# Eight Toeplitz products per middle block instead of ten, and the second block's residual in four pieces

## Chip, core and metric

The kernel runs on one core of a Trainium2 chip. The metric is the device time of one execution in microseconds (us). Before the change the median of three runs is 409.83 us, from 409.52 to 410.25 us.

## What is computed

The input is 2 x 1024 rows of 512 float32 values. Each row is normalised. One branch convolves it causally with a learned kernel K of 512 taps (an S4 layer, whose K is built on the chip from small complex vectors); the other is a gated feed-forward layer with low-rank (LoRA) additions to its weights. The result is their product added to the input:

```python
xn = _layernorm(x, axis=-1)
# s: causal convolution of xn with K along the 512 values, plus D * xn
y = jnp.fft.irfft(jnp.fft.rfft(u, n=n) * jnp.fft.rfft(K, n=n), n=n)[..., :L]
s = y + D[0] * u
# g: silu of the feed-forward layer
h1 = _lora_linear(x, w1, lora_A1, lora_B1)
h3 = _lora_linear(x, w3, lora_A3, lora_B3)
f = _lora_linear(silu(h1) * h3, w2, lora_A2, lora_B2)
x = x + s * silu(f)
```

## The kernel before

The 2048 rows are worked on in four blocks of 512 rows. Features lie on the partitions, in four chunks of 128 (c = 0 to 3), and rows along the free axis. A float32 product is made of three matmuls on values split into a high and a low part (fp32r): low weights by high data, high weights by low data, high by high. The function `three` issues them, and its three lines in the profile are L991, L992 and L993. Each streams 512 columns.

**A block.** The 1376 hidden units are 11 tiles, j = 0 to 10. For a tile TensorE makes `gate` into bank h1 (12 matmuls), `up` into bank h3 (12 matmuls), and then `down(j-1)`, the product of the previous tile's hidden values with w2, into four banks f (12 matmuls). Between them ScalarE applies silu to h1 (L651), VectorE multiplies by h3 (L837), ScalarE makes the high part `ghl[0]` with a cast (`hidden_hi`, L668) and VectorE the low part `ghl[1]` with a subtraction (`hidden_lo`, L842). There is one buffer `ghl`, so `hidden_hi` of tile j waits on the semaphore g_used until `down(j-1)` has read it. Each engine runs its instructions in the order of its own program; in the bodies of ScalarE and VectorE that order is told by the places "gate", "up" and "down" of each j. `hidden_lo(j)` stands at (j, "up").

**The convolution.** K is 512 taps, so the convolution is a lower triangular Toeplitz matrix of 4 x 4 chunks. With T0 to T3 for its four different chunks, kept split in `tzs`, output chunk c is the sum of T(c-i) by x(i) for i = 0 to c: 4 + 3 + 2 + 1 = 10 products, 30 matmuls. `convolve` makes them at the end of each block, into the banks h1, h3, spare1 and spare0, among the last `down` products (`down_chunk` of tile 10). `out_sum` on VectorE multiplies them with silu of f and adds the residual `xres`.

**Blocks.** Block 0 is written out and also builds the folded weights: raw tiles of w1, w3 and w2 are loaded, a low-rank product from TensorE is added, and the sum is split. Blocks 1 and 2, the middle blocks, are one loop body, and block 3 is written out. The next block's data is prepared during a block: moments on VectorE (L792, L795), their reciprocal roots on GpSimd (`rows_rstd`), a store and a broadcast load of the scales, `next_scale` on GpSimd (four tensor_tensor of 128x512), `next_shift` on VectorE (L819), the high part on ScalarE (L637) and the low part on VectorE (`next_lo`, L823).

**Queues.** Nearly all loads are issued by SyncE (SP) in one written order. The residual of block 1 is one transfer of 1 MB (`load_residual(1, 1)`), issued ahead of the last six raw weight tiles; `next_scale(1, 1)` waits for it. At the end of a middle block SP stores the four output chunks, and then loads the rows of the next but one.

Of the kernel before, what the change touches and what calls it, by code (L numbers as in the profile page):

```python
# [25 lines left out]
ALU = mybir.AluOpType  # L26
# [18 lines left out]

COS, MASK, SIGN, MINUS_HALF, EULER, MINUS_ONE, EPSILON, EYE = 0, 8, 10, 11, 13, 14, 18, 20

# [163 lines left out]


def spare_uses():
# [32 lines left out]
def s4_constants():  # L246

    L = D  # L250
    lane = np.arange(L // 2)
    mirror = np.where(lane == 0, L // 2, L - lane)
    l = np.concatenate([lane, mirror])
    half = np.pi * l / L
    trig = np.concatenate([np.sin(half), np.cos(half)])[None, :].astype(np.float32)
    cosc = np.repeat(np.cos(half).reshape(4, P).T, 2, axis=1)
    mask = np.ones((P, 2))
    mask[0, 0] = 0.0
    sign = np.where(np.arange(P) < NS, 1.0, -1.0)[:, None]
    powers = np.tile([-0.5, -0.5, np.e, -1.0, -1.0, -1.0, -1.0, EPS, EPS], (P, 1))  # L260
    lanes = np.concatenate([cosc, mask, sign, powers, np.eye(P)], axis=1).astype(np.float32)
    t = np.arange(L) + 0.5
    lc, ls = lane, np.where(lane == 0, L // 2, lane)
    cos_rows = np.cos(2 * np.pi * ((lc[:, None] * t[None, :]) % L) / L) / L
    sin_rows = -np.sin(2 * np.pi * ((ls[:, None] * t[None, :]) % L) / L) / L
    dft = np.stack([cos_rows, sin_rows]).reshape(2, 2, P, P, K_PARTS).transpose(3, 4, 0, 2, 1).reshape(P, K_PARTS, L).astype(np.float32)
    return trig, lanes, np.ascontiguousarray(dft)


def build(nc, x, xT, w1, w3, w2, lora, lora_early, lora_late, s4_lanes, s4_vc, s4_bp, s4_scalars, trig, lanes, dft, outT):  # L270
    ctx = ExitStack()
    with ctx:
# [25 lines left out]
        xn = put("xn", [P, RT, D])  # L298
        g = put("g", [P, BLK])
        tz = put("tz", [P, D])  # L300
        lane_c = put("lane_c", [P, EYE + P])
# [3 lines left out]
        scales = put("scales", [P, 2, RT])  # L305
        bp_sb = put("bp_sb", [P, NS])
        scal = put("scal", [P, 2])
# [8 lines left out]
        coef = put("coef", [P, 4])  # L316
        kcol = put("kcol", [P, K_PARTS])
        assert base + top[0] <= nc.sbuf_usable_end

# [26 lines left out]
        rows_next = at("rows_next", [P, 2, D], lora_off + (DC + 2) * BLK * 4)  # L346
        scale_rows = at("scale_rows", [P, 2, BLK], lora_off + (DC + 4) * BLK * 4)
        assert lora_off + (DC + 6) * BLK * 4 <= xn_off

# [63 lines left out]
        s4_step = sem("s4_step")  # L413
        pads_cleared = sem("pads_cleared")


# [79 lines left out]
        def wait_residual(eng, b):  # L496
            if isinstance(b, int) and b == 0:
                eng.wait_ge(res0_in, 16)
            else:
                eng.wait_ge(res_in, 16 * b)  # L500

# [9 lines left out]
        def _(sync):  # L511
# [111 lines left out]
        def _(act):  # L623
# [61 lines left out]
            def out_gate(b):  # L685
                for n, c in enumerate(OUT_ORDER):
# [4 lines left out]
                    nc.scalar.activation(gate[:, n % 2, :], f[c][:, :], ACT.Silu).then_inc(gate_done, 1)  # L691

            def body(b, par_next, first, last):
                norm_at = NORM_AT_FIRST if first else NORM_AT
# [29 lines left out]
                if last:  # L724
                    last_gate(b)
                else:
                    out_gate(b)


# [28 lines left out]
        def _(dve):  # L758
# [86 lines left out]
            def last_sum(b, par):  # L845
# [3 lines left out]
                for i, (n, out, cols) in enumerate(steps):  # L849
                    part = gate_last(n)[:, cols]  # L850
                    dve.wait_ge(gate_done, b * DC + n + 1)
                    dve.wait_ge(conv_ready, b * DC + i + 1)
# [3 lines left out]
                    nc.vector.tensor_tensor(sum_, sum_, part, ALU.add).then_inc(res_done, 1)  # L856

            def out_sum(b, par):
# [13 lines left out]
            def body(b, par, par_next, first, last):  # L872
                norm_at = NORM_AT_FIRST if first else NORM_AT
                split_at = SPLIT_AT_FIRST if first else SPLIT_AT
                moments_at = MOMENTS_AT_FIRST if first else MOMENTS_AT
                late = []
# [45 lines left out]
                if last:  # L922
                    last_sum(b, par)
                else:
                    out_sum(b, par)
# [28 lines left out]
        def _(pe):  # L954
# [118 lines left out]
            def convolve(b, par, c_out, first):  # L1073
# [12 lines left out]
                mm.then_inc(conv_ready, 1)  # L1086

            def convolve_halves(b, par, c_out):

# [22 lines left out]
            def body(b, par, first, last):  # L1112
                if first:
                    start()
                for j in range(1 if first else 0, HT):
# [5 lines left out]
                    else:  # L1121
                        pe.wait_ge(conv_used, (b - 1) * DC + 1)
                    if j == HT - 1:
# [9 lines left out]
                    else:  # L1133
                        pe.wait_ge(conv_used, (b - 1) * DC + 2)
                    if j == HT - 1:
# [41 lines left out]
        def _(pool):  # L1177
# [28 lines left out]
            def next_scale(b, par):  # L1206

                pool.wait_ge(scale_rows_in, 16 * b)
                pool.wait_ge(res_in, 16 * b)
                for c in range(DC):  # L1210
# [137 lines left out]
            pool.wait_ge(wlo_done, len(DVE_LO))  # L1348
            next_scale(1, 1)
            with pool.Fori(1, NBLK - 1) as b:  # L1350
                for r in range(0, RT, 2):
                    rows_rstd(b + 1, r)
                pool.wait_ge(conv_ready, b * DC)
                next_scale(b + 1, (b + 1) % 2)
# [55 lines left out]
```

## Time and profile before

| | value |
|---|---|
| median of 3 runs (range) | 409.83 us (409.52 to 410.25) |
| profiled execution | 409.98 us |
| its span in the trace | 408.2 us |
| mean granted TensorE clock | 0.999 of full speed |
| busy: TensorE / its weight loads / VectorE / ScalarE / GpSimd | 403.3 / 335.8 / 170.1 / 105.9 / 73.3 us |

The span is the stretch from the first to the last instruction in the trace, and lies 1.8 us under the execution's own time. The busy time of TensorE counts each matmul from its start to its modelled end; one matmul's end lies behind the next one's start, so the cost of a matmul is read from start to start. PE is TensorE, PEld its weight loads, DVE VectorE, ACT ScalarE, POOL GpSimd and SP SyncE.

### The profile page before, as it was taken

To read this page: it belongs to the slowest core of one execution; us is meant where nothing else is said; L and a number is where in the kernel's file an instruction comes from. 1 tells how busy PE (TensorE), PEld (TensorE's weight loads), DVE (VectorE), ACT (ScalarE), POOL (GpSimd) and SP (SyncE) were. 2 spreads that over 40 slices of the span, in tenths; PEclk is the share of its full clock that TensorE was granted. 3 is DMA by queue.
4 is the path that set the end of the run, shared out by engine and by line. 5 is a ranking of instruction groups with operands and counts; after the bars stand their busy time and mean duration, and the time that the engine had idled before them with its cause. 6 is when DMAs were issued, how large, how long until landed. Compare 5 with 4: busy or idle time off the path is not lost.

```text
span 408.2 us, 5004 instructions
## 1 busy us (share of the span) xinstructions
PE 403.3 (99%) x1850; PEld 335.8 (82%) x1850; DVE 170.1 (42%) x267; ACT 105.9 (26%) x175; POOL 73.3 (18%) x139
## 2 busy tenths in 40 slices
PE   8999999999999999999999999999999999999996
PEld 8988888887788888888888888888888888888885
DVE  5887776794793322232343221233234111211125
ACT  7554232222351111221221111112222111111122
POOL 6685645402500114000000103300000000000000
PEclk9999999999999999999999999999999999999999
DMA  8573755604425101000016101000002000000002
GB/s 269 166 184 108 231 156 152 171 26 90 145 78 180 52 2 51 2 0 0 2 51 205 53 0 52 0 0 0 0 0 103 2 0 0 2 0 0 2 0 103
DMA packets 14466, 26.89 MB, mean 66 GB/s; under 512 B 2768, under 2 KB 4528, under 8 KB 14320
## 3 DMA queue, kind: packets, MB, share of 16 engines
q1 hardware_dynamic: 13440, 24.53, 19.2%
q0 software_dynamic: 720, 1.60, 2.0%
q10 hardware_dynamic: 288, 0.52, 0.3%
q8 instruction: 11, 0.18, 0.2%
q14 instruction: 7, 0.06, 0.1%
HBM read 21.45 MB, written 4.54 MB: 64 GB/s over the span
## 4 chain that ended last, share of the span: by engine, by line
PE 94%; DVE 3%; issue 1%; DMA 1%; ACT 1%; POOL 0%; DVEq 0%; POOLq 0%
PE h L991 20%; PE h L992 20%; PE h L993 20%; PE f L991 10%; PE f L992 10%; PE f L993 10%; PE h L1014 2%; PE spare L978 1%; DMA xn<-x_dram 1%; DVE raw L768 1%; PE spare L993 1%; PE spare L973 1%; PE spare L992 1%; PE spare L991 1%; DVE w L783 0%
## 5 line engine op out<-in xcount | busy, mean ns | idle before, releaser
L991 PE MATMUL h<-xt,w 128*128 (+2 forms) x340 | 131.4, 386 | 0.0
L992 PE MATMUL h<-xt,w 128*128 (+2 forms) x340 | 131.2, 386 | 0.0
L993 PE MATMUL h<-xt,w 128*128 (+2 forms) x340 | 131.2, 386 | 0.0
L991 PEld LDWEIGHTS h<-xt,w 128*128 128x128 f32 x340 | 63.9, 188 | 13.3 <-DVE w L780 0.4
L993 PEld LDWEIGHTS h<-xt,w 128*128 128x128 f32 x340 | 63.9, 188 | 12.9
L992 PEld LDWEIGHTS h<-xt,w 128*128 128x128 f32 x340 | 63.9, 188 | 12.3
L837 DVE TENSOR_TENSOR g<-g,h 128x512 f32<-128x512 f32 x40 | 27.5, 686 | 106.3 <-PE h L993 106.1
L842 DVE TENSOR_TENSOR ghl<-g,ghl 128x512 fp32r<-128x512 f32 x44 | 32.4, 736 | 90.0 <-ACT ghl L668 90.0
L991 PE MATMUL f<-ghl,w2f 128*128 128x512 f32 x176 | 68.8, 391 | 0.0
L992 PE MATMUL f<-ghl,w2f 128*128 128x512 f32 x176 | 68.6, 390 | 0.0
L993 PE MATMUL f<-ghl,w2f 128*128 128x512 f32 x176 | 68.5, 389 | 0.0
L668 ACT CAST ghl<-g 128x512 fp32r<-128x512 f32 x44 | 27.3, 621 | 155.6 <-PE f L993 145.0
L991 PEld LDWEIGHTS f<-ghl,w2f 128*128 128x128 f32 x176 | 33.0, 188 | 7.0 <-issue 0.4
L993 PEld LDWEIGHTS f<-ghl,w2f 128*128 128x128 f32 x176 | 33.1, 188 | 7.0
L992 PEld LDWEIGHTS f<-ghl,w2f 128*128 128x128 f32 x176 | 33.1, 188 | 6.5
L651 ACT ACTIVATE g<-h 128x512 f32<-128x512 f32 x40 | 23.9, 597 | 44.9 <-PE h L993 44.9
L1190 POOL TENSOR_TENSOR scales<-moments,lane_c 128x2 f32<-128x2 f32 x6 | 1.5, 256 | 120.6 <-DVE moments L795 120.6
L768 DVE SCALAR_TENSOR_TENSOR raw<-spare,raw 128x512 f32<-128x512 f32 (+2 forms) x33 | 22.3, 675 | 2.0 <-DVE raw L768 1.1
L628 ACT CAST w<-raw 128x512 fp32r<-128x512 f32 (+1 forms) x22 | 13.4, 610 | 30.4 <-DVE raw L768 30.4
L1190 POOL TENSOR_TENSOR normal_rows<-xres,scale_rows 128x512 f32 (+1 forms) x12 | 16.1, 1372 | 19.8 <-DMA scale_rows<-scales_scratch 19.8
L783 DVE TENSOR_TENSOR w<-raw,w 128x512 fp32r<-128x512 f32 (+1 forms) x17 | 13.0, 772 | 0.3 <-DVE raw L768 0.2
L637 ACT CAST xt<-normal_rows (+1 forms) x12 | 7.4, 621 | 16.4 <-DVE normal_rows L819 16.4
(141 smaller groups left out, 310.4 us busy)
## 6 DMA issues: line engine op xcount, KB each, us to landing
raw<-w_dram SPq DMA_DIRECT2D x28, 256.0 KB, 3.9
xres<-xT_dram SPq DMA_DIRECT2D x4, 1024.0 KB, 6.9
outT_dram<-xres SPq DMA_DIRECT2D x15, 256.0 KB, 2.5
rows_next<-x_dram SPq DMA_DIRECT2D x4, 512.0 KB, 3.6
scale_rows<-scales_scratch SPq DMA_DIRECT2D x3, 512.0 KB, 4.2
rows<-x_dram SPq DMA_DIRECT2D x2, 512.0 KB, 7.1
dft_sb<-dft_dram SPq DMA_DIRECT2D x1, 1024.0 KB, 5.0
raw<-w_dram SPq DMA_DIRECT2D x4, 224.0 KB, 3.2
```

The costliest lines, as they stand in the source:

```text
L628: nc.scalar.copy(folded(kind, j, 0), raw_tile(kind, j)).then_inc(whi_done, 1)
L651: nc.scalar.activation(g[:, :], h1[:, :], ACT.Silu).then_inc(silu_done, 1)
L668: nc.scalar.copy(ghl[:, 0, :], g[:, :]).then_inc(ghi_done, 1)
L768: nc.vector.scalar_tensor_tensor(out=rt, in0=low, scalar=LORA_SCALE, in1=rt, op0=ALU.mult, op1=ALU.add) \
L783: nc.vector.tensor_tensor(folded(kind, j, 1), raw_tile(kind, j), folded(kind, j, 0).bitcast(F32), ALU.subtract).then_inc(wlo_done, 1)
L837: nc.vector.tensor_tensor(g[:, :], g[:, :], h3[:, :], ALU.mult).then_inc(g_done, 1)
L842: nc.vector.tensor_tensor(ghl[:, 1, :], g[:, :], ghl[:, 0, :].bitcast(F32), ALU.subtract).then_inc(glo_done, 1)
L991: pe.matmul(out, w[1], m[0], start=start, stop=False)
L992: pe.matmul(out, w[0], m[1], start=False, stop=False)
L993: return pe.matmul(out, w[0], m[0], start=False, stop=stop)
L1014: mm = pe.matmul(h3[:, :], joint[:, c, JOINT_APART:JOINT_APART + P], xt[:, par, hl, c, :], start=(c == 0 and hl == 1), stop=(c == DC - 1 a ...
L1190: return nc.gpsimd.tensor_tensor(out, a, c, op)
```

## The change

In blocks 1 and 2 the ten products are replaced by eight, in the manner of Karatsuba. With P0 = T0 x0, P1 = T1 x1 and P2 = T2 x2, the chunks are

- y0 = P0
- y1 = (T0+T1)(x0+x1) - P0 - P1
- y2 = (T0+T2)(x0+x2) - P0 - P2 + P1
- y3 = T3 x0 + T0 x3 + (T1+T2)(x1+x2) - P1 - P2

TensorE makes them at four places of the block (`products`, behind `down(j-1)` of j = 2, 4, 5 and 6) and at its end (`last_product`). VectorE forms the sums of x (`pair_sum`: three additions each), ScalarE casts them (`pair_high`), VectorE subtracts (`pair_low`), and `mix` combines the products. The sums of T are formed once, on GpSimd and ScalarE, between block 0 and block 1. Blocks 0 and 3 keep their ten products. The load of block 1's residual becomes four transfers of 256 KB, each behind one of the raw tiles.

The diff, without the allocations, the semaphores and the wait counts of the last block:

```diff
+MIX_AT = {(3, "gate"): (0,), (5, "gate"): (1,), (6, "gate"): (2,), (7, "gate"): (3,)}
+PAIRS = ((0, 1), (0, 2), (1, 2))
+PAIR_AT, PAIR_LO_AT = {(4, "gate"): 0, (5, "gate"): 1, (7, "gate"): 2}, {(4, "up"): 0, (5, "up"): 1, (7, "up"): 2}
...
 @@ sync
+            def load_residual_part(c):
+                sync.dma_start(resid(1, c), xT[:, c, BLK:2 * BLK]).then_inc(res_in, 16)
...
             sync.wait_ge(xt_turned, RT)
-            load_residual(1, 1)
-            for kind, j in later[17:]:
+            for n, (kind, j) in enumerate(later[17:]):
                 load_raw(kind, j)
+                if n < DC:
+                    load_residual_part(n)
...
 @@ scalar
+            def pair_high(b, k):
+                act.wait_ge(pair_step, 9 * b - 9 + 3 * k + 3)
+                nc.scalar.copy(pair_hi[:, :], pair_f[:, :]).then_inc(pair_cast, 1)
+            def mid_gate(b):
+                for n, c in enumerate(OUT_ORDER):
+                    e = b * DC + n
+                    act.wait_ge(f_ready, e + 1)
+                    act.wait_ge(res_done, e - 1)
+                    nc.scalar.activation(scale_rows[:, n % 2, :], f[c][:, :], ACT.Silu).then_inc(gate_done, 1)
...
                         if place == "gate" and not (first and j == 0):
                             hidden(b, j)
+                        if mid and (j, place) in PAIR_AT:
+                            if PAIR_AT[j, place] == 0:
+                                act.wait_ge(tsum_done, 2)
+                            pair_high(b, PAIR_AT[j, place])
...
                 else:
                     out_gate(b)
+                    act.wait_ge(tsum_added, 2)
+                    nc.scalar.copy(tsum[:, 0, :, :], tsum_f[:, :, :]).then_inc(tsum_hi, 1)
+                    nc.scalar.copy(t12_hi[:, :], t12_f[:, :]).then_inc(tsum_hi, 1)
...
 @@ vector
+            def pair_sum(b, par, k):
+                lo, hi = [[xt[:, par, hl, c, :].bitcast(F32) for c in PAIRS[k]] for hl in (1, 0)]
+                n = 9 * b - 9 + 3 * k
+                whole = pair_f[:, :]
+                nc.vector.tensor_tensor(whole, lo[0], lo[1], ALU.add).then_inc(pair_step, 1)
...
+                nc.vector.tensor_tensor(whole, whole, hi[0], ALU.add).then_inc(pair_step, 1)
...
+                nc.vector.tensor_tensor(whole, whole, hi[1], ALU.add).then_inc(pair_step, 1)
+            def pair_low(b, k):
+                dve.wait_ge(pair_cast, 3 * b - 3 + k + 1)
+                nc.vector.tensor_tensor(pair_lo[:, :], pair_f[:, :], pair_hi[:, :].bitcast(F32), ALU.subtract) \
+                    .then_inc(pair_ready, 1)
+            def mix(b, stage):
+                p, m, s = PRODUCTS * b - PRODUCTS, PRODUCTS * b - PRODUCTS, 3 * b - 3
+                dve.wait_ge(prod_ready, p + stage + 1)
+                if stage == 0:
+                    nc.vector.tensor_copy(y2, sp[1][:, :]).then_inc(mix_step, 1)
...
+                    nc.vector.tensor_tensor(y1, sp[0][:, :], y2, ALU.add).then_inc(mix_done, 1)
...
+            def mid_sum(b, par):
+                mix(b, 4)
+                dve.wait_ge(mix_done, PRODUCTS * b)
+                wait_residual(dve, b)
+                sums = {3: less, 2: y2, 1: y1, 0: sp[0][:, :]}
...
                     for place in ("gate", "up", "down"):
+                        if mid:
+                            for stage in MIX_AT.get((j, place), ()):
+                                mix(b, stage)
+                            if (j, place) in PAIR_AT:
+                                pair_sum(b, par, PAIR_AT[j, place])
                         if place == "up" and not (first and j == 0):
                             hidden_mul(b, j)
...
                         if place == "up":
                             hidden_lo(b, j)
+                        if mid and (j, place) in PAIR_LO_AT:
+                            pair_low(b, PAIR_LO_AT[j, place])
...
 @@ tensor
+            def paired(b, k, out, start, stop):
+                pe.wait_ge(pair_ready, 3 * b - 3 + k + 1)
+                t = [t12_hi[:, :], t12_lo[:, :]] if k == 2 else [tsum[:, hl, k, :] for hl in (0, 1)]
+                return three(out, t, [pair_hi[:, :], pair_lo[:, :]], start, stop)
+            def products(b, par, j):
+                m = PRODUCTS * b - PRODUCTS
+                if j == 2:
+                    single(b, par, 0, take(b, ("conv", b, 0), False)[:, :])
+                    single(b, par, 1, take(b, ("conv", b, 1), False)[:, :]).then_inc(prod_ready, 1)
+                if j == 4:
+                    pe.wait_ge(mix_done, m + 1)
+                    pe.wait_ge(tsum_done, 2)
+                    paired(b, 0, sp[1][:, :], True, True).then_inc(prod_ready, 1)
+                if j == 5:
+                    pe.wait_ge(mix_done, m + 2)
+                    single(b, par, 2, sp[1][:, :]).then_inc(prod_ready, 1)
+                if j == 6:
+                    pe.wait_ge(mix_done, m + 3)
+                    paired(b, 1, sp[1][:, :], True, True).then_inc(prod_ready, 1)
+            def last_product(b, par):
+                pe.wait_ge(mix_done, PRODUCTS * b - PRODUCTS + 4)
+                three(sp[1][:, :], lag(3), [xt[:, par, hl, 0, :] for hl in (0, 1)], True, False)
+                three(sp[1][:, :], lag(0), [xt[:, par, hl, 3, :] for hl in (0, 1)], False, False)
+                paired(b, 2, sp[1][:, :], False, True).then_inc(prod_ready, 1)
...
                         down(b, j - 1)
                     if first:
                         extras(j, "down")
+                    elif not last:
+                        products(b, par, j)
...
+                if not first:
+                    last_product(b, par)
+                    down_wait(b, HT - 1)
+                    for c in OUT_ORDER:
+                        down_chunk(HT - 1, c).then_inc(f_ready, 1)
+                    return
...
 @@ gpsimd
             next_scale(1, 1)
+            pool.wait_ge(tz_in, 16)
+            once = tz[:, 0:P].rearrange("p (a l) -> p a l", a=1).to_broadcast([P, 2, P])
+            tt(tsum_f[:, :, :], tz[:, P:3 * P].rearrange("p (a l) -> p a l", a=2), once, ALU.add).then_inc(tsum_added, 1)
+            tt(t12_f[:, :], tz[:, P:2 * P], tz[:, 2 * P:3 * P], ALU.add).then_inc(tsum_added, 1)
+            pool.wait_ge(tsum_hi, 2)
+            tt(tsum[:, 1, :, :], tsum_f[:, :, :], tsum[:, 0, :, :].bitcast(F32), ALU.subtract).then_inc(tsum_done, 1)
+            tt(t12_lo[:, :], t12_f[:, :], t12_hi[:, :].bitcast(F32), ALU.subtract).then_inc(tsum_done, 1)
```

## Rows read from the trace of the kernel before

**Rows 1.** The page, busy time by engine (share of the span) and TensorE's granted clock in 40 slices

```profile
PE 403.3 (99%) x1850; PEld 335.8 (82%) x1850; DVE 170.1 (42%) x267; ACT 105.9 (26%) x175; POOL 73.3 (18%) x139
...
PEclk9999999999999999999999999999999999999999
```

**Rows 2.** Windows of blocks 1 and 2: start:end, length, busy (count), clock, DMA share, GB/s

```profile
117.73:213.28 95.55, 95.55 (x423) 79.12 (x422) 31.22 (x51) 20.43 (x34) 7.63 (x12) 1.00 0.13 42
213.28:308.93 95.65, 95.65 (x423) 79.22 (x422) 29.23 (x48) 19.35 (x33) 7.60 (x12) 1.00 0.12 39
```

**Rows 3.** Waits of block 2: who waited for whom, total us, times, longest

```profile
ACT ghl L668 <- PE f L993: 45.7, 10, 4.8
```

**Rows 4.** Timeline in block 2, TensorE, ScalarE and VectorE where down(3) ends: start, us, instruction

```profile
251.36 0.39 PE L991 MATMUL h<-xt,w 128*128 x1
...
251.56 0.62 ACT L668 CAST ghl<-g 128x512 fp32r<-128x512 f32 x1 [4.84 <-PE f L993]
...
252.22 0.69 DVE L842 TENSOR_TENSOR ghl<-g,ghl 128x512 fp32r<-128x512 f32 x1 [2.62 <-ACT ghl L668]
```

**Rows 5.** Timeline of VectorE in block 2, hidden_lo(5) with the next instruction behind it

```profile
260.38 0.69 DVE L842 TENSOR_TENSOR ghl<-g,ghl 128x512 fp32r<-128x512 f32 x1 [2.62 <-ACT ghl L668]
260.99 0.69 DVE L819 TENSOR_TENSOR normal_rows<-normal_rows,scale_rows 128x512 f32 x1
```

**Rows 6.** Timeline in block 0 where TensorE waits for VectorE

```profile
94.08 0.28 DVE L780 TENSOR_TENSOR w<-raw,w 128x128 fp32r<-128x128 f32 x1
...
94.46 0.47 PE L991 MATMUL h<-xt,w 128*128 128x512 f32 x1
...
94.77 0.39 PE L992 MATMUL h<-xt,w 128*128 128x512 f32 x1
```

**Rows 7.** Timeline of GpSimd, its next_scale in block 0 and in block 2

```profile
108.66 1.29 POOL L1190 TENSOR_TENSOR normal_rows<-xres,scale_rows 128x512 f32<-128x512 f32 x1
109.91 1.74 POOL L1190 TENSOR_TENSOR normal_rows<-xres,scale_rows 128x512 f32<-128x512 f32 x1
...
253.31 5.04 POOL L1190 TENSOR_TENSOR normal_rows<-xres,scale_rows 128x512 f32 x4 [6.03 <-DMA scale_rows<-scales_scratch]
```

**Rows 8.** Timeline of VectorE at the end of block 0

```profile
108.68 1.82 DVE L842 TENSOR_TENSOR ghl<-g,ghl 128x512 fp32r<-128x512 f32 x1 [1.14 <-ACT ghl L668]
110.42 1.77 DVE L819 TENSOR_TENSOR normal_rows<-normal_rows,scale_rows 128x512 f32<-128x512 f32 x1
112.11 0.68 DVE L819 TENSOR_TENSOR normal_rows<-normal_rows,scale_rows 128x512 f32<-128x512 f32 x1
...
116.50 0.68 DVE L863 TENSOR_TENSOR gate<-gate,h 128x512 f32<-128x512 f32 x1
```

**Rows 9.** Timeline of TensorE at the first instruction of block 1

```profile
117.48 0.19 PEld L991 LDWEIGHTS h<-xt,w 128*128 128x128 f32 x1 [0.17 <-issue]
117.57 0.41 PE L991 MATMUL h<-xt,w 128*128 x1
```

**Rows 10.** Timeline at the end of block 1: tile 10's low part, TensorE's first convolution and down_chunk

```profile
204.62 0.69 DVE L842 TENSOR_TENSOR ghl<-g,ghl 128x512 fp32r<-128x512 f32 x1 [0.91 <-ACT ghl L668]
...
203.76 0.39 PE L991 MATMUL h<-xt,tzs 128*128 x1
...
206.48 0.39 PE L991 MATMUL f<-ghl,w2f 128*128 128x512 f32 x1
```

**Rows 11.** Timeline of VectorE across the boundary at 213.28: out_sum and the next block's first product

```profile
210.71 0.69 DVE L863 TENSOR_TENSOR gate<-gate,h 128x512 f32<-128x512 f32 x1 [0.95 <-ACT gate L691]
211.54 0.69 DVE L869 TENSOR_TENSOR xres<-xres,gate 128x512 f32 x1
...
218.99 0.69 DVE L837 TENSOR_TENSOR g<-g,h 128x512 f32<-128x512 f32 x1 [3.04 <-PE h L993]
```

**Rows 12.** Timeline of the SP queue in block 0 around the residual of block 1

```profile
67.06 0.66 SPq L548 DMA_DIRECT2D xres<-xT_dram  x1
69.05 27.66 SPq L543 DMA_DIRECT2D raw<-w_dram  x6
```

More of the change, by code:

```diff
@@ L260, in s4_constants @@
     powers = np.tile([-0.5, -0.5, np.e, -1.0, -1.0, -1.0, -1.0, EPS, EPS], (P, 1))
-    lanes = np.concatenate([cosc, mask, sign, powers, np.eye(P)], axis=1).astype(np.float32)
+    lanes = np.concatenate([cosc, mask, sign, powers, np.ones((P, 4)), np.eye(P)], axis=1).astype(np.float32)
     t = np.arange(L) + 0.5
@@ L299, in build @@
         g = put("g", [P, BLK])
+        tz_off = (top[0] + 31) // 32 * 32
         tz = put("tz", [P, D])
+        lane_c_off = (top[0] + 31) // 32 * 32
         lane_c = put("lane_c", [P, EYE + P])
@@ L317, in build @@
         kcol = put("kcol", [P, K_PARTS])
+        assert bp_off + P * 4 <= top[0]
+        sum_off = (top[0] + 31) // 32 * 32
+        tsum = put("tsum", [P, 2, 2, P], F32R)
+        tsum_f = at("tsum_whole", [P, 2, P], sum_off + 2 * P * 4)
+        t12_hi = at("t12_hi", [P, P], lane_c_off + EYE * 4, F32R)
+        t12_lo = at("t12_lo", [P, P], bp_off, F32R)
+        t12_f = at("t12_whole", [P, P], bp_off)
         assert base + top[0] <= nc.sbuf_usable_end
@@ L347, in build @@
         scale_rows = at("scale_rows", [P, 2, BLK], lora_off + (DC + 4) * BLK * 4)
+        pair_f = at("pair_whole", [P, BLK], lora_off + (DC + 3) * BLK * 4)
+        pair_lo = at("pair_lo", [P, BLK], lora_off + (DC + 3) * BLK * 4, F32R)
+        pair_hi = at("pair_hi", [P, BLK], tz_off, F32R)
+        y1, y2, less = gate[:, 0, :], gate[:, 1, :], rows_next[:, 0, :]
         assert lora_off + (DC + 6) * BLK * 4 <= xn_off
@@ L414, in build @@
         pads_cleared = sem("pads_cleared")
+        tsum_added, tsum_hi, tsum_done = sem("tsum_added"), sem("tsum_hi"), sem("tsum_done")
+        prod_ready, mix_step, mix_done = sem("prod_ready"), sem("mix_step"), sem("mix_done")
+        pair_step, pair_cast, pair_ready = sem("pair_step"), sem("pair_cast"), sem("pair_ready")
         joint = w13[:, W13_AT[1, JOINT] // 4:W13_BYTES // 4].rearrange("p (c u) -> p c u", c=DC)
@@ L691, in out_gate @@
                     nc.scalar.activation(gate[:, n % 2, :], f[c][:, :], ACT.Silu).then_inc(gate_done, 1)
+            def pair_high(b, k):
[7 more added lines that the diff above has]
+                    nc.scalar.activation(scale_rows[:, n % 2, :], f[c][:, :], ACT.Silu).then_inc(gate_done, 1)
             def body(b, par_next, first, last):
+                mid = not first and not last
                 norm_at = NORM_AT_FIRST if first else NORM_AT
@@ new lines, in pair_low @@
+            def pair_low(b, k):
[7 more added lines that the diff above has]
+                    nc.vector.tensor_copy(y2, sp[1][:, :]).then_inc(mix_step, 1)
+                    dve.wait_ge(mix_step, s + 1)
+                    nc.vector.tensor_tensor(y1, sp[0][:, :], y2, ALU.add).then_inc(mix_done, 1)
+                if stage == 1:
+                    dve.wait_ge(mix_done, m + 1)
+                    nc.vector.tensor_tensor(y1, sp[1][:, :], y1, ALU.subtract).then_inc(mix_done, 1)
+                if stage == 2:
+                    nc.vector.tensor_tensor(less, y2, sp[1][:, :], ALU.add).then_inc(mix_step, 1)
+                    nc.vector.tensor_tensor(y2, y2, sp[1][:, :], ALU.subtract).then_inc(mix_done, 1)
+                    dve.wait_ge(mix_done, m + 3)
+                    nc.vector.tensor_tensor(y2, y2, sp[0][:, :], ALU.subtract).then_inc(mix_step, 1)
+                if stage == 3:
+                    dve.wait_ge(mix_step, s + 3)
+                    nc.vector.tensor_tensor(y2, y2, sp[1][:, :], ALU.add).then_inc(mix_done, 1)
+                if stage == 4:
+                    dve.wait_ge(mix_step, s + 3)
+                    nc.vector.tensor_tensor(less, sp[1][:, :], less, ALU.subtract).then_inc(mix_done, 1)
@@ new lines, in mid_sum @@
+            def mid_sum(b, par):
[3 more added lines that the diff above has]
+                sums = {3: less, 2: y2, 1: y1, 0: sp[0][:, :]}
+                for n, c in enumerate(OUT_ORDER):
+                    e = b * DC + n
+                    part = scale_rows[:, n % 2, :]
+                    dve.wait_ge(gate_done, e + 1)
+                    nc.vector.tensor_tensor(part, part, sums[c], ALU.mult).then_inc(conv_used, 1)
+                    dve.wait_ge(conv_used, e + 1)
+                    if c < 2:
+                        dve.sem_inc(spare_free[c], 1)
+                    nc.vector.tensor_tensor(resid(par, c), resid(par, c), part, ALU.add).then_inc(res_done, 1)
@@ L875, in body @@
                 moments_at = MOMENTS_AT_FIRST if first else MOMENTS_AT
+                mid = not first and not last
                 late = []
@@ L923, in body @@
                     last_sum(b, par)
+                elif mid:
+                    mid_sum(b, par)
                 else:
@@ L1086, in convolve, with lag, single @@
                 mm.then_inc(conv_ready, 1)
+            def lag(d):
+                return [tzs[:, hl, d * P:(d + 1) * P] for hl in (0, 1)]
+            def single(b, par, d, out):
+                return three(out, lag(d), [xt[:, par, hl, d, :] for hl in (0, 1)], True, True)
+            def paired(b, k, out, start, stop):
[22 more added lines that the diff above has]
+                paired(b, 2, sp[1][:, :], False, True).then_inc(prod_ready, 1)
             def convolve_halves(b, par, c_out):
```

22 lines of the change are left out of this document (15 added, 7 removed).

## Prediction

> **What bounds the kernel.** I read the page's busy times first: TensorE is busy 99% of the span at the full granted clock in every slice, VectorE 42%, ScalarE 26%, GpSimd 18% [rows 1]. A busy share alone does not show that TensorE is fed without gaps, because its matmuls overlap in the record. So I took the windows of the two middle blocks next. They are bounded by the starts of two successive first matmuls, and in the second, 95.65 us hold 422 weight loads [rows 2]: 95.65 / 422 = 0.2267 us from matmul to matmul. The same spacing stands in the timeline wherever I looked in these blocks, so block 2 has no idle time of TensorE at all. The consequence for the reader is double. Every matmul taken out of such a block is worth 0.227 us, and every wait put in front of a matmul is paid in full, unless it is moved under other matmuls: nothing in the block absorbs it. So the question of this change is only whether the new operands are ready when TensorE comes to them.
>
> **What is removed.** Ten products become eight, each of three matmuls: 6 matmuls a block, 12 in all, 12 x 0.2267 = 2.72 us less. (The Trainium skill, page "TensorE: Matmul & The Clock Gate", section "Back-to-back issue gap", gives about 216 ns for an isolated gap of 512 columns and 131 ns for a sustained stream; by the latter the twelve would be worth 1.57 us. The rows here show 227 ns, and decide.)
>
> **What is added on TensorE's path: the first paired product.** For each product I compared the point in TensorE's program with the point at which its operand is made.
>
> `paired(0)` stands right behind `down(3)`, in `products` of j = 4. It waits for pair_ready, which `pair_low` increments. `pair_low(0)` stands on VectorE at (4, "up"), behind `hidden_lo(4)`, and that waits for the cast of `hidden_hi(4)`. The cast waits for g_used, since `ghl` is a single buffer: it can't run before `down(3)` has read it. The waits show just this: ten times in the block the cast waits for TensorE's f product, 4.8 us at the longest [rows 3]. In the timeline the matmul behind `down(3)` starts at 251.36 and the cast at 251.56 [rows 4]. So where before the next matmul (gate of tile 5) needed nothing of this chain, TensorE now waits for all of it. The links, from the moment at which the next matmul would have started:
>
> - to the start of the cast 251.56 - 251.36 = 0.20 us, and from the cast to the subtraction 252.22 - 251.56 = 0.66 us [rows 4]
> - from `hidden_lo` to the next instruction of VectorE 260.99 - 260.38 = 0.61 us, which now is `pair_low`, and 0.69 us for it, as a tensor_tensor of the same form takes [rows 5]
> - from VectorE's end to TensorE's matmul 94.46 - 94.36 = 0.10 us, and 0.31 instead of 0.23 us to the second matmul after a wait, 0.08 us [rows 6]
>
> Together 2.34 us in each middle block, 4.68 us in all. The nearest bounds: without the restart 2.26 us a block; with `pair_low` behind one instruction of GpSimd, 3.5 us (rival B). What hangs behind the stall shifts as a whole, because the chain of later tiles starts from TensorE too.
>
> **The other products are covered.** `single` 0 and 1 at j = 2 need only x. `mix(0)` then has the gate and up products of tile 3 (24 matmuls, 5.4 us) before VectorE must multiply by h3. `single(2)` at j = 5 waits for `mix(1)`, which has a whole tile (36 matmuls, 8.16 us). `pair_sum(1)` and `mix(1)` are four instructions of 0.69 us, 2.8 us with some 0.1 us between them, and VectorE owes nothing to tile 5 until its gate and up products are through, 5.4 us after the stall. `paired(1)` needs `pair_low(1)`, made behind `down(4)`, and is used behind `down(5)`: 8.16 us for some 2.3 us. `paired(2)` has three tiles. So they cost nothing as long as VectorE is not late by more than a tile.
>
> **End of a block.** Tile 10's low part is ready at 204.62 + 0.69 = 205.31, and `down(9)` gives way at 203.76. Before, 12 matmuls of convolution covered that until 206.48 [rows 10]. Now nine do, until 203.76 + 9 x 0.2267 = 205.80: the wait stays covered with 0.5 us to spare. `mid_sum` starts later against the block's end, since all four f products come last: four pairs of instructions at some 1.5 us (0.83 us from product to sum, then the next), from about 1.2 us before the boundary to 4.9 us after it. The next thing VectorE has to do is at 218.99, 5.7 us after 213.28 [rows 11]. Covered, and if not, the h3 bank isn't needed before 8.2 us. SP's stores and the next rows' load come about 2 us later; the rows are read by moments that nobody needs for several tiles.
>
> **Between blocks 0 and 1: the sums of T.** GpSimd adds 256 and 128 columns right behind `next_scale(1, 1)`, which ends at 109.91 + 1.74 = 111.65 [rows 7], while VectorE works without a pause toward L863, which ends at 117.18. TensorE's first load of block 1 waits for that product (h1 is a convolution bank there) and starts at 117.48 [rows 9]: 0.30 us of slack. Where GpSimd's 512-column instructions overlap VectorE's with two SBUF inputs, these take 1.82 and 1.77 us instead of 0.68 or 0.69, about 1.1 us more each, and end about when GpSimd's do [rows 7, 8]. Scaled by columns, the two new ones cost VectorE 0.55 + 0.28 = 0.83 us. Less the slack, plus 0.1 us of restart, TensorE loses 0.6 us, once. Bounds: 0 if they fall in gaps; 1.9 us if both cost as much as one of 512 columns. I take the scaled value, since the length of an elementwise instruction goes with its columns. (The Trainium skill, page "SBUF — State Buffer", section "Who interferes with whom", has a rule against this change: a VectorE instruction with two SBUF inputs and a GpSimd one that reads SBUF exclude each other for a whole instruction. The trace agrees: 1.82 against 0.69 us. Without that rule the term would be 0.) The casts on ScalarE and GpSimd's subtractions come behind `out_gate(0)` and are wanted at j = 4 of block 1, 30 us later.
>
> **The residual in pieces.** The 1 MB transfer goes out at 67.06, and the six raw tiles from 69.05 to 96.7 [rows 12]; their issues wait for earlier splits. The pieces go out behind the first four, the last one before the sixth tile at 96.7, and GpSimd reads the residual in the `next_scale` that is under way at 108.66 [rows 7]. The view of waits lists no fold that waited for a raw tile's transfer, so the raw tiles gain nothing by coming sooner. Zero, hidden on both sides.
>
> **Sum.** -2.72 + 4.68 + 0.6 = +2.56 us. Against the profiled execution's 409.98 us this is 412.54; that execution lies 0.15 us above the median, so I forecast 412.4 us.
>
> **Rivals.**
>
> - A, the forecast: a stall of some 2.3 us in each middle block, 412.4 us, by its own bounds 411.2 to 413.7. Chance 0.76.
> - B, `pair_low(0)` is caught behind GpSimd. It starts at 252.22 + 0.61 = 252.83, and `next_scale` at 253.31 [rows 7]; both keep their place relative to `down(2)` and `down(3)`, so `pair_low` is first by 0.5 us. If scales land earlier, it loses 1.1 us in each block: 414.6 us. Chance 0.08.
> - C, the granted clock falls after the stall. The clock is full in every slice [rows 1], but no middle block shows an idle TensorE, so no row speaks to 2.3 us. At half the clock, 12 matmuls cost 2.72 us more, in both blocks 5.4 us: 417.8 us, more if it lasts. Against it: block 0 has short waits at a full clock. Chance 0.05.
> - D, the other side: the operand is there in time and the change does what it says. Then -2.72 + 0.6 gives 407.7 us. It would need VectorE to run `pair_low(0)` ahead of `hidden_lo(4)`, or the cast not to wait for `down(3)`; program order and [rows 3] speak against both. It decides as soon as the chain costs less than (2.72 - 0.6) / 2 = 1.06 us a block, less than cast and subtraction alone. Chance 0.07.
> - E, a smaller stall for a reason I don't see, about even with before. Chance 0.04.
>
> **Numbers.** The range 411.2 to 414.0 holds A and the nearer half of B, 0.80. A measurement of this kernel tells about 0.2%, 0.8 us, from no change. Slower by more than that: A, B, C, 0.89. Faster: D, 0.07. Within: E, 0.04.
>
> **What the profile after would show.** The middle blocks hold 416 weight loads instead of 422 and last 95.65 - 1.36 + 2.34 = 96.6 us. TensorE has one idle stretch of about 2.3 us in each, in front of the first matmul that reads `tsum`, with VectorE's `pair_low` as releaser, and none at j = 2, 5, 6 or the end. The first load of block 1 comes some 0.6 us later against the end of block 0, with L863 delayed by GpSimd's additions. The forecast is wrong if `pair_low(0)` ends before `down(3)` does, or if a second idle stretch appears in the block.

## The result and the profile after

The changed kernel takes 415.16 us in the median of six runs (413.62 to 415.93), the kernel before 409.77 us in its six. The ratio is 1.0115, with a 95% interval of 1.0097 to 1.0133: 4.7 us slower, 4.0 to 5.4. The two medians lie 5.4 us apart, at the upper end of that. The forecast was 412.4 us in a range of 411.2 to 414.0: the direction was right, and the measured median lies 2.8 us above the forecast. Two slow executions among the experiments, of 446.5 us (experiment 1, clock 0.852) and 1054.6 us (experiment 2), are left out of the ratios.

The page of the profiled execution (415.93 us, span 414.1 us), its busy times and TensorE's granted clock:

```profile
PE 405.0 (98%) x1838; PEld 336.5 (81%) x1838; DVE 200.0 (48%) x307; ACT 110.0 (27%) x183; POOL 81.3 (20%) x143
...
PEclk9999999999999998999999999899999999999999
```

Against [rows 1] twelve matmuls are gone, VectorE is busy for 30 us more, and the clock, full in every slice before, has two slices with an 8. The view of waits of TensorE, in total us, times, longest (pair_lo is written by `pair_low`, gate by L972):

```profile
PE spare L1110 <- DVE pair_lo L926: 4.1, 2, 2.0
PE h L1141 <- POOL g L1376: 1.0, 1, 1.0
PE h L1110 <- DVE gate L972: 0.7, 1, 0.7
```

The wait for GpSimd's g stands in the kernel before too, with the same 1.0 us. The two new waits, the first and the third, are the ones that the forecast named. The first, in block 1, in the timeline of TensorE, ScalarE and VectorE (L702 is the cast, L897 hidden_lo, L926 pair_low, L1110 to L1112 the three lines of `three`):

```profile
157.38 0.39 PE L1112 MATMUL f<-ghl,w2f 128*128 128x512 f32 x1
159.80 0.50 PE L1110 MATMUL spare<-pair_hi,tsum 128*128 128x512 f32 x1 [2.03 <-DVE pair_lo L926]
160.14 0.40 PE L1111 MATMUL spare<-pair_lo,tsum 128*128 128x512 f32 x1
...
157.81 0.62 ACT L702 CAST ghl<-g 128x512 fp32r<-128x512 f32 x1 [2.71 <-PE f L1112]
...
158.46 0.69 DVE L897 TENSOR_TENSOR ghl<-g,ghl 128x512 fp32r<-128x512 f32 x1 [2.61 <-ACT ghl L702]
159.06 0.68 DVE L926 TENSOR_TENSOR pair_lo<-pair_whole,pair_hi 128x512 fp32r<-128x512 f32 x1
```

The next matmul would have started at 157.38 + 0.23 = 157.61. It starts at 159.80, 2.19 us late, and the second one comes 0.34 us behind it in place of 0.23: 2.30 us. The chain is cast, subtraction, subtraction, as in [rows 4, 5]. Block 2 repeats it to the hundredth.

What the sum did not hold comes just after the product, in the timeline of TensorE, in block 1 and then in block 2:

```profile
160.38 0.41 PE L1112 MATMUL spare<-pair_hi,tsum 128*128 128x512 f32 x1
160.61 0.60 PE L1110 MATMUL h<-xt,w 128*128 x1
161.01 0.63 PE L1111 MATMUL h<-xt,w 128*128 x1
...
163.57 0.61 PE L1111 MATMUL h<-xt,w 128*128 x1
163.99 0.42 PE L1112 MATMUL h<-xt,w 128*128 x1
164.25 0.40 PE L1110 MATMUL h<-xt,w 128*128 x1
```

```profile
258.14 0.50 PE L1110 MATMUL spare<-pair_hi,tsum 128*128 128x512 f32 x1 [2.03 <-DVE pair_lo L926]
...
259.41 0.44 PE L1112 MATMUL h<-xt,w 128*128 x1
259.65 0.63 PE L1110 MATMUL h<-xt,w 128*128 x1
260.07 0.63 PE L1111 MATMUL h<-xt,w 128*128 x1
```

From 160.61 to 163.99 eight matmuls start 0.40 to 0.43 us apart instead of 0.23. They read the same tiles with the same columns as in [rows 4]. The slow stretch does not begin when the wait ends: it begins 0.8 us after the product's first matmul in block 1 and 1.5 us after it in block 2 (259.65 - 258.14), and the matmuls in between come at the usual spacing. Windows of that stretch and of the two middle blocks (length, busy times, clock):

```profile
160.58:164.36 3.78, 3.78 (x11) 2.93 (x10) 3.36 (x4) 0.00 (x0) 3.78 (x3) 0.55 0.00 0
...
118.01:216.51 98.50, 96.47 (x417) 79.27 (x417) 43.87 (x67) 21.47 (x37) 10.58 (x14) 0.98 0.12 38
216.51:314.87 98.36, 96.33 (x417) 79.13 (x416) 44.41 (x68) 21.13 (x35) 9.32 (x12) 0.98 0.11 37
```

The granted clock of the stretch is 0.55: for most of it TensorE ran at the lower of its two levels, 1.2 GHz, after an idle stretch of 2.0 us. The blocks last 98.50 and 98.36 us. Against the forecast 96.6 us, each is 1.8 to 1.9 us longer. Most of that is the slow stretch: in both blocks the 30 matmuls behind the product's first take 1.8 us more than 30 x 0.2267 us, and in the block of the third run that kept its clock (experiment 7) 0.14 us more. So one fall of the clock costs 1.6 us.

The start of block 1, and VectorE and GpSimd ahead of it:

```profile
118.01 0.50 PE L1110 MATMUL h<-xt,w 128*128 x1 [0.68 <-DVE gate L972]
...
109.20 3.48 DVE L874 TENSOR_TENSOR normal_rows<-normal_rows,scale_rows 128x512 f32<-128x512 f32 x2
112.61 1.22 DVE L878 TENSOR_TENSOR xt<-normal_rows,xt 128x512 fp32r<-128x512 f32 x1
...
117.03 0.68 DVE L972 TENSOR_TENSOR gate<-gate,h 128x512 f32<-128x512 f32 x1
...
112.09 1.19 POOL L1353 TENSOR_TENSOR tsum_whole<-tz 128x256 f32<-128x256 f32 x1
113.24 0.91 POOL L1353 TENSOR_TENSOR t_whole<-tz 128x128 f32<-128x128 f32 x1
```

GpSimd's two additions lie at 112.09 and 113.24, L972 starts at 117.03 instead of 116.50 [rows 8], and block 1 at 118.01 instead of 117.57 [rows 9].

With that the whole difference of the two profiled executions is placed. The window of block 1 in [rows 2] opens 0.16 us after the block's first matmul. From first matmul to first matmul it lasts 213.28 - 117.57 = 95.71 us. Block 1 starts 0.44 us later, lasts 98.50 - 95.71 = 2.79 us longer, and block 2 lasts 98.36 - 95.65 = 2.71 us longer. That is 5.94 of the 5.95 us between 409.98 and 415.93.

### The profile page after: what moved, and what is told of

Its sections match the earlier page's. It is cut to its first block, busy times and chain, and to the rows that moved or that the text cites. A ratio compares the mean times of both kernels' runs of the same rounds, so it can differ in the third digit from the quotient of the medians.

```text
span 414.1 us, 5084 instructions
## 1 busy us (share of the span) xinstructions
PE 405.0 (98%) x1838; PEld 336.5 (81%) x1838; DVE 200.0 (48%) x307; ACT 110.0 (27%) x183; POOL 81.3 (20%) x143
## 4 chain that ended last, share of the span: by engine, by line
PE 92%; DVE 4%; ACT 1%; issue 1%; DMA 1%; POOL 0%; DVEq 0%; ACTq 0%; POOLq 0%
PE h L1110 19%; PE h L1111 19%; PE h L1112 19%; PE f L1110 9%; PE f L1111 9%; PE f L1112 9%; PE h L1133 2%; PE spare L1097 1%; DVE normal_rows L874 1%; PE spare L1110 1%; PE spare L1112 1%; PE spare L1111 1%; DMA xn<-x_dram 1%; PE spare L1092 1%; DVE xt L878 1%
## 5 line engine op out<-in xcount | busy, mean ns | idle before, releaser
L1110 PE MATMUL h<-xt,w 128*128 (+2 forms) x340 | 132.9, 391 | 0.7 <-DVE gate L972 0.7
L1112 PE MATMUL h<-xt,w 128*128 (+2 forms) x340 | 132.2, 389 | 0.0
L1110 PEld LDWEIGHTS h<-xt,w 128*128 128x128 f32 x340 | 64.5, 190 | 14.7 <-issue 1.1
L1112 PEld LDWEIGHTS h<-xt,w 128*128 128x128 f32 x340 | 64.7, 190 | 13.3
L1111 PEld LDWEIGHTS h<-xt,w 128*128 128x128 f32 x340 | 64.7, 190 | 12.7
L897 DVE TENSOR_TENSOR ghl<-g,ghl 128x512 fp32r<-128x512 f32 x44 | 31.0, 704 | 90.4 <-ACT ghl L702 90.4
L1110 PE MATMUL f<-ghl,w2f 128*128 128x512 f32 x176 | 68.7, 390 | 0.0
L1112 PE MATMUL f<-ghl,w2f 128*128 128x512 f32 x176 | 68.5, 389 | 0.0
L702 ACT CAST ghl<-g 128x512 fp32r<-128x512 f32 x44 | 27.3, 621 | 145.6 <-PE f L1112 135.0
L1112 PEld LDWEIGHTS f<-ghl,w2f 128*128 128x128 f32 x176 | 33.0, 188 | 7.0
L1110 PEld LDWEIGHTS f<-ghl,w2f 128*128 128x128 f32 x176 | 33.0, 188 | 6.7
L1353 POOL TENSOR_TENSOR normal_rows<-xres,scale_rows 128x512 f32 (+1 forms) x12 | 19.2, 1628 | 20.7 <-DMA scale_rows<-scales_scratch 20.7
```

What stands on the lines that cost most here:

```text
L702: nc.scalar.copy(ghl[:, 0, :], g[:, :]).then_inc(ghi_done, 1)
L897: nc.vector.tensor_tensor(ghl[:, 1, :], g[:, :], ghl[:, 0, :].bitcast(F32), ALU.subtract).then_inc(glo_done, 1)
L1110: pe.matmul(out, w[1], m[0], start=start, stop=False)
L1111: pe.matmul(out, w[0], m[1], start=False, stop=False)
L1112: return pe.matmul(out, w[0], m[0], start=False, stop=stop)
L1353: return nc.gpsimd.tensor_tensor(out, a, c, op)
```

## Experiments

All ten kernels are timed against the kernel before, in up to five rounds. Where a number of executions by clock is given, it is the mean granted clock that each execution's record shows.

**1. The operand ahead of the cast.** One instruction of the change is moved on VectorE:

```diff
+                        if mid and (j, place) == (4, "up"):
+                            pair_low(b, 0)
                         if place == "up" and not (first and j == 0):
                             hidden_mul(b, j)
...
-                        if mid and (j, place) in PAIR_LO_AT:
+                        if mid and (j, place) in PAIR_LO_AT and j != 4:
```

> The change, with one instruction moved: VectorE runs pair_low(0) at (4, "up") ahead of hidden_mul(4), so that it no longer stands behind the cast of tile 4. Theory A (a stall of 2.30 us in each middle block for pair_low, and behind it some nine matmuls at 0.43 instead of 0.23 us): both vanish together, TensorE idles nowhere in the middle blocks, the granted clock stays full, and the time is that of before -2.72 us for twelve matmuls +0.44 us for GpSimd's additions, about 2.3 us under before. Rival (VectorE or GpSimd are now too loaded and would hold TensorE elsewhere): another idle stretch appears and the time stays at or above that of before.

Measured: ratio 0.9953 (0.9940 to 0.9965), 1.9 us faster than before, 1.4 to 2.5. Its timeline, VectorE and TensorE in block 1:

```profile
154.25 0.69 DVE L926 TENSOR_TENSOR pair_lo<-pair_whole,pair_hi 128x512 fp32r<-128x512 f32 x1 [0.69 <-ACT pair_hi L729]
154.86 0.68 DVE L892 TENSOR_TENSOR g<-g,h 128x512 f32<-128x512 f32 x1
157.59 0.69 DVE L897 TENSOR_TENSOR ghl<-g,ghl 128x512 fp32r<-128x512 f32 x1 [2.04 <-ACT ghl L702]
...
156.50 0.40 PE L1114 MATMUL f<-ghl,w2f 128*128 128x512 f32 x1
156.74 0.39 PE L1112 MATMUL spare<-pair_hi,tsum 128*128 128x512 f32 x1
```

`pair_low` ends at 154.94, and the product follows `down(3)` at the usual spacing, 156.50 to 156.74. The executions in the comparison kept a clock of 0.999 or 1.000. So the place of one subtraction of 0.69 us is the whole difference between 4.7 us slower and 1.9 us faster. The other products and the end of the block put no idle stretch into the middle blocks. This order is the one that rival D of the forecast supposed: it gave 407.7 us, 2.1 us under before.

**2. The idle stretch filled.** Eight matmuls whose result is overwritten:

```diff
                     pe.wait_ge(tsum_done, 2)
+                    for _ in range(8):
+                        pe.matmul(sp[1][:, :], tzs[:, 0, 0:P], xt[:, par, 0, 0, :], start=True, stop=True)
                     paired(b, 0, sp[1][:, :], True, True).then_inc(prod_ready, 1)
```

> The change, with eight extra matmuls of 512 columns into the spare1 bank in front of the wait for pair_low(0); their results are overwritten by the product. They take 1.8 us of the 2.3 us in which TensorE idled. Theory that the fall of the granted clock is a cost of its own, caused by the idle stretch: the stall ends at the same moment, the clock stays full in every execution, and the time is 1.5 to 3.5 us under that of the change, 2.2 to 2.7 us over before. Rival (the slow matmuls come from the reads of the pair or of tsum, or from VectorE's and GpSimd's load, and not from the idle stretch): the matmuls behind the product stay slow and the time is that of the change, 5.4 us over before.

Measured: 1.0065 (1.0052 to 1.0078), 2.7 us slower than before, 2.1 to 3.2. TensorE in its block 2:

```profile
255.70 0.50 PE L1110 MATMUL spare<-pair_hi,tsum 128*128 128x512 f32 x1 [0.23 <-DVE pair_lo L926]
...
257.19 0.40 PE L1110 MATMUL h<-xt,w 128*128 x1
257.42 0.39 PE L1111 MATMUL h<-xt,w 128*128 x1
```

The wait is still there, now 0.23 us of idling behind 1.8 us of filler. The same product, operands and gate matmuls follow, and none is slow in either block; the executions in the comparison show 0.999 or 1.000. Matmuls whose results nobody uses make the changed kernel about 2 us faster. That settles two things: the slow matmuls come from the idle stretch, not from the operands; and without a fall of the clock the change costs 2.7 us, where the forecast had summed 2.56.

**3. and 4. The wait without the change.** The kernel before, with one line. First behind `down(3)`, then behind `down(2)`:

```diff
+                    elif not last and j == 4:
+                        pe.wait_ge(glo_done, b * HT + 5)
```

> The kernel before, with nothing of the change but a wait: behind down(3) in the middle blocks TensorE waits for hidden_lo(4). The links read before give 0.20 + 0.66 + 0.69 + 0.18 = 1.7 us a block. Theory A without a fall of the clock: 3.4 us over before. If so short an idle stretch lowers the granted clock too, up to 1.75 us more in each block, 5 to 7 us over before. Rival (something downstream absorbs the wait): under 2 us over before.

```diff
+                    elif not last and j == 3:
+                        pe.wait_ge(moments_ready, (b + 1) * RT + RT)
```

> The kernel before, with nothing of the change but a longer wait: behind down(2) in the middle blocks TensorE waits for the moments that VectorE takes behind hidden_lo(3), 2.6 us a block, a little more than the 2.3 us of the change. Stall alone: 5.3 us over before. Stall and clock: the granted clock falls behind it as in the change, 1.75 us a block more where it does, up to 8.8 us over before. Rival (the fall of the clock belongs to the paired product's operands): the clock stays full and the time is 5.3 us over before.

Measured: 1.0097 (1.0082 to 1.0112) for the short wait, 4.0 us slower, 3.4 to 4.6; and 1.0172 (1.0145 to 1.0200) for the long one, 7.0 us, 5.9 to 8.2. The matmuls around each wait, in block 1, the short wait first:

```profile
155.66 0.39 PE L993 MATMUL f<-ghl,w2f 128*128 128x512 f32 x1
157.48 0.50 PE L991 MATMUL h<-xt,w 128*128 x1 [1.43 <-DVE ghl L842]
157.81 0.39 PE L992 MATMUL h<-xt,w 128*128 x1
```

```profile
147.24 0.39 PE L993 MATMUL f<-ghl,w2f 128*128 128x512 f32 x1
150.08 0.49 PE L991 MATMUL h<-xt,w 128*128 x1 [2.45 <-DVE moments L795]
150.41 0.40 PE L992 MATMUL h<-xt,w 128*128 x1
```

The short wait costs 157.48 - 155.66 - 0.23 + 0.10 = 1.69 us a block, 3.4 us in all, at the lower end of what the times say; the traces show nothing that would make it 4.0. The long wait costs 150.08 - 147.24 - 0.23 + 0.10 = 2.71 us a block. All four executions with the short wait kept a clock of 1.000. The six with the long one fall on steps: three at 1.000 took 414.8 to 415.4 us, one at 0.996 took 417.0, two at 0.992 took 418.2 and 418.4. The three at 1.000 are 5.4 us over before, twice 2.7; each step down is some 1.6 us, the price of one fall as read above. The kept trace is of an execution at 1.000 and has no slow matmul, so the steps are read from times and mean clocks alone. A wait is paid in full here, and the loss of clock is a second, separate cost that comes in some executions. It needs nothing of the Toeplitz products.

**5. Less filling.** As experiment 2, with `range(3)`, so that 1.36 us stay idle.

> The change with three extra matmuls ahead of the wait for pair_low(0) in place of eight, so that TensorE idles 1.4 to 1.6 us in each middle block instead of 2.0 us. The stall ends at the same moment, so the time without a fall of the clock is that of the version with eight, 412.3 us. Theory that the length of the idle stretch decides about the clock, as the pure wait of 1.6 us without a fall suggests: the clock stays full in all or nearly all executions. Rival (any wait in this place can lower it): executions at 0.991 to 0.996 and a median of 413.5 us or more.

Measured: 1.0075 (1.0061 to 1.0089), 3.1 us slower, 2.5 to 3.6. Four executions at 1.000 took 412.1 to 412.7 us, one at 0.998 took 413.2. None fell to 0.996. The one at 0.998 is 0.5 to 1.1 us over the others; executions of the kernel before at 0.998 took 409.4 to 409.8 us, no more than the rest, so it is open whether that one holds a short fall. In the other four, three matmuls in the gap were enough to keep the clock.

**6. and 7. The change again, twice.**

> The change as it is, once more. Theory A with the clock: two stalls of 2.3 us and GpSimd's term of 0.4 us give 2.3 us over before in an execution whose granted clock stays full, and each fall of the clock adds 1.1 to 1.8 us, so that the executions fall on steps by their mean granted clock (1.000, 0.996, 0.991). Rival: executions at 1.000 also lie more than 3 us over before, and something beside stall and clock costs time.

> The change a third time, for more executions at each mean granted clock. One execution so far kept the full clock and yet took 413.6 us, where stall and GpSimd's term alone give 412.3 us, which is what the version with eight filling matmuls took. Theory A with the clock: further executions at 1.000 lie near 412.3 us, those at 0.995 near 414.2 us and those at 0.991 near 415.7 us. Rival: executions at 1.000 lie at 413.6 us again, and 1.3 us have another cause.

Measured: 1.0101 (1.0085 to 1.0116) and 1.0110 (1.0094 to 1.0125). By their ratios these two are 4.1 and 4.5 us slower than before. With the first six, 14 executions of the change are now sorted by clock: four at 0.990 or 0.991 took 415.5 to 415.9 us, nine at 0.994 to 0.996 took 413.5 to 414.7 us, and one at 1.000 took 413.6 us. The profile of the last run shows one fall, so both prices are in one trace. Windows of its two middle blocks:

```profile
117.48:215.93 98.45, 96.42 (x417) 79.27 (x417) 44.66 (x67) 21.57 (x37) 10.06 (x14) 0.98 0.12 38
215.93:312.66 96.73, 94.69 (x418) 78.03 (x417) 44.21 (x68) 21.11 (x35) 9.35 (x12) 1.00 0.12 38
```

Both blocks have the stall of 2.04 us idle. The one with a full clock lasts 96.73 us, and the forecast for it was 96.6. The one with the fall lasts 1.72 us more. Some 0.1 us of that is the late second matmul at the start of block 1 and not the fall: in experiment 1, which has no fall, block 1 lasts 94.51 us and block 2 94.40. The expectation that executions at 1.000 would be near 412.3 us could not be tried again, as none came; the one at 413.6 us is not explained.

**8. The product one step later on TensorE.** VectorE and ScalarE keep the order of the change; `paired(0)` goes from behind `down(3)` to behind the gate product of tile 5:

```diff
-                if j == 4:
-                    pe.wait_ge(mix_done, m + 1)
-                    pe.wait_ge(tsum_done, 2)
-                    paired(b, 0, sp[1][:, :], True, True).then_inc(prod_ready, 1)
...
                     if first:
                         extras(j, "gate")
+                    elif not last and j == 5:
+                        pe.wait_ge(mix_done, PRODUCTS * b - PRODUCTS + 1)
+                        pe.wait_ge(tsum_done, 2)
+                        paired(b, 0, sp[1][:, :], True, True).then_inc(prod_ready, 1)
```

> The change with paired(0) moved on TensorE from behind down(3) to behind the gate product of tile 5; VectorE and ScalarE keep their order. The 12 matmuls of that gate product are 2.72 us of cover for a chain of 2.26 us. Theory A: no idle stretch at the product, full clock, and the time of the version with pair_low(0) moved, 2.0 us under before. Rival (what delays the product is the operand's own making, not the place): TensorE idles there by the same 2.0 us.

Measured: 0.9945 (0.9932 to 0.9959), 2.3 us faster than before. Its timeline, VectorE and TensorE:

```profile
158.50 0.69 DVE L926 TENSOR_TENSOR pair_lo<-pair_whole,pair_hi 128x512 fp32r<-128x512 f32 x1
...
159.53 0.40 PE L1112 MATMUL h<-xt,w 128*128 x1
159.77 0.39 PE L1110 MATMUL spare<-pair_hi,tsum 128*128 128x512 f32 x1
```

The chain is as late as in the change, `pair_low` ends at 159.19, and the product follows at 159.77 without a gap. So the operand need not be made sooner; 12 matmuls between its source and its use do as well.

**9. GpSimd's additions ahead of next_scale.** Experiment 1, with the wait for tz_in and the two additions moved ahead of `next_scale(1, 1)`:

```diff
+            pool.wait_ge(tz_in, 16)
+            once = tz[:, 0:P].rearrange("p (a l) -> p a l", a=1).to_broadcast([P, 2, P])
+            tt(tsum_f[:, :, :], tz[:, P:3 * P].rearrange("p (a l) -> p a l", a=2), once, ALU.add).then_inc(tsum_added, 1)
+            tt(t12_f[:, :], tz[:, P:2 * P], tz[:, 2 * P:3 * P], ALU.add).then_inc(tsum_added, 1)
             pool.wait_ge(shift_ready, RT // 2)
             pool.wait_ge(wlo_done, len(DVE_LO))
             next_scale(1, 1)
...
```

> The change with pair_low(0) ahead of hidden_mul(4), and GpSimd's two additions of the sums of T ahead of next_scale(1, 1) in place of behind it, in the time in which it waits for the scales. Theory (the additions delay VectorE's L972 by 0.4 to 0.6 us past TensorE's slack at the start of block 1): the first matmul of block 1 comes 0.4 us sooner than with pair_low(0) moved alone, 2.5 us under before. Rival (the start of block 1 is set by something else): no difference from it, 2.0 us under before.

Measured: 0.9943 (0.9929 to 0.9956), 2.3 us faster than before, 1.8 to 2.9. Its timelines of GpSimd and TensorE:

```profile
101.88 0.73 POOL L1355 TENSOR_TENSOR tsum_whole<-tz 128x256 f32<-128x256 f32 x1 [3.54 <-DMA tz<-k_scratch]
102.57 0.46 POOL L1355 TENSOR_TENSOR t_whole<-tz 128x128 f32<-128x128 f32 x1
...
117.31 0.39 PE L1114 MATMUL spare<-xt,tzs 128*128 128x512 f32 x1
117.54 0.39 PE L1112 MATMUL h<-xt,w 128*128 x1
```

Windows of its two middle blocks:

```profile
117.54:211.94 94.40, 94.40 (x418) 78.10 (x416) 43.59 (x67) 21.62 (x37) 10.38 (x14) 1.00 0.12 40
211.94:306.34 94.40, 94.40 (x418) 78.10 (x416) 44.26 (x68) 21.17 (x35) 8.90 (x12) 1.00 0.12 39
```

The additions take 0.73 and 0.46 us instead of 1.19 and 0.91, and block 1 starts without a gap, 117.31 to 117.54. The traces with the additions behind `next_scale` idle there by different amounts: 0.2 us in experiment 1 and in the third run of the change (0.41 and 0.42 us between starts), 0.8 us in the first profile of the change (1.07 us), and amounts in between in the other traces. In time, experiments 1 and 9 cannot be told apart: their intervals overlap over more than half their length. Experiment 9 is level with experiment 8 as the fastest version made.

**10. The pieces alone.** The kernel before, with only the residual in four pieces (the wait counts of the residual are raised to match, not shown):

```diff
-            load_residual(1, 1)
-            for kind, j in later[17:]:
+            for n, (kind, j) in enumerate(later[17:]):
                 load_raw(kind, j)
+                if n < DC:
+                    load_residual_part(n)
```

> The kernel before with the residual of block 1 in four pieces, and nothing else of the change. Theory: no fold waits for a raw tile, so nothing moves, within 0.2 us of before. Rival (the raw tiles come sooner and block 0 shortens, or the pieces delay the k chain): more than 0.5 us either way, to be seen at the first matmul of block 1.

Measured: 1.0001 (0.9992 to 1.0010). Nothing, as expected.

## Why the prediction was right about the stall and wrong about the clock

- **What bounds the kernel**: right. Waits are paid in full (experiments 3 and 4) and matmuls come at 0.2267 us. The removed six are worth nearly what was forecast: in experiment 9, with no stall and no fall, both middle blocks last 94.40 us against 95.65, 1.25 us a block for 1.36. Experiments 1, 8 and 9 gain 1.9 to 2.3 us (1.4 to 2.9 by their intervals).
- **The first paired product**: right, in place, releaser and size. Forecast 2.34 us a block, measured 2.30 us.
- **The other products and the block's end**: right. In the trace of the change the low part of tile 10 ends at 213.22 and `down_chunk` starts at 213.75, 0.5 us to spare as forecast. VectorE's last sum ends 5.3 us behind the boundary (forecast 4.9), 0.45 us before the next thing VectorE has to do. `pair_sum(1)` ran into GpSimd's `next_scale`: two additions took 1.65 and 1.55 us instead of 0.69, where nothing waited.
- **The sums of T**: forecast 0.6 us, a gap of 0.2 to 0.8 us in the traces, too small for the times to confirm. The mechanism, GpSimd's additions ahead of L972, is borne out by the gap's absence in experiment 9.
- **The residual in pieces**: right, zero (experiment 10).
- **What failed is the sum's missing term, rival C.** The sum put the cost of the clock behind the stall at nothing, and the forecast gave a fall of the granted clock a chance of 0.05, on the ground that block 0's short waits left the clock full. Those waits are a few tenths of a microsecond and say nothing about 2.3. By the mean clock of the executions, and by the three traces kept, it fell once or twice in 13 of 14 executions of the change. Its price in C, 12 matmuls and 2.72 us a fall, was too high: it is eight or nine matmuls and 1.6 us. With two falls the sum reads 409.98 - 2.72 + 4.60 + 0.6 + 2 x 1.6 = 415.7 us, and the profiled execution took 415.93. The likeliest case, A, is a state that the kernel hardly ever took. Experiment 2 built it, at 2.7 us over before.
- **The range** had a lower bound below its own terms: 409.83 - 2.72 + 2 x 2.26 with nothing for GpSimd is 411.6 us, not 411.2. The upper bound, 414.0, had no room for two falls of 1.6 us on top of 412.4.

Left open: the single execution of the change at a full clock that took 413.6 us; and why the clock falls in some executions and not in others. The length of the idle stretch alone doesn't order it: two stretches of 2.04 us lowered the clock at least once in 13 of 14 executions, two of 2.45 us in 3 of 6, two of 1.43 us in none of 4, two of 1.36 us in none of 5 clearly.

## What to carry to other kernels

Before putting an operand's last step on an engine, look at what the instruction in front of it waits for, and whether that is the very instruction behind which the operand is used. Here a subtraction stood behind a cast that could not start before `down(3)` had ended, and its product stood right behind `down(3)`; moving either by one step turned 4.7 us slower into some 2 us faster.

Where TensorE is saturated as here, price an idle stretch of two microseconds twice: its own length, and a possible stretch of matmuls at the lower clock behind it. If the trace of before has no idle stretch of that length, it gives no evidence that the clock will stay, and the second price belongs in the range.

## What the runs showed of the hardware

The granted clock fell after 2.04 us without a matmul, in stretches otherwise wholly busy, for eight or nine matmuls of 512 columns, and not in every execution. In the three traces that show it, the first slow matmul starts 0.6 to 1.5 us after the idle stretch has ended. Three filler matmuls, which cut the idle time to 1.36 us, kept the mean clock at 0.998 or more. (The Trainium skill, page "SBUF — State Buffer", section "Who interferes with whom", says that a VectorE instruction with two SBUF inputs and a GpSimd one that reads SBUF exclude each other. The trace agrees: beside `next_scale` two such additions took 1.65 and 1.55 us, and GpSimd's addition of 256 columns took 1.19 us beside VectorE's L874 and L878 and 0.73 us ahead of them, in experiment 9.)
